# A graph-attention kernel: dense edge weights as relu(A·B − 1) in PSUM by ScalarE, the units' one-hots by VectorE in one pass

## The reference

```python
hs, hd = h[src], h[dst]
e = jnp.concatenate([hs, hd], axis=1)
a1 = jnp.exp(jax.nn.relu(e @ W_att_1 + b_att_1))          # a2, a3 likewise
att1 = jax.ops.segment_sum(a1, dst, num_segments=N)
avg_a = (a1 / att1[dst] + a2 / att2[dst] + a3 / att3[dst]) / 3.0
m = avg_a * relu(relu(relu(hs @ W_msg_1 + b_msg_1) @ W_msg_2 + b_msg_2) @ W_msg_3 + b_msg_3)
h_neigh = jax.ops.segment_sum(m, dst, num_segments=N) / jnp.maximum(deg, 1.0)
out = relu(jnp.concatenate([h, h_neigh], axis=1) @ W_c1 + b_c1) @ W_c2 + b_c2
x = _layernorm(x + out)
```

## Time and profile before

| | us |
|---|---|
| median of 3 runs (784.7 to 786.55) | 785.11 |
| the profiled execution, its own time | 788.37 |
| its span (first to last instruction) | 784.4 |
| PE busy | 635.0 (81%) |
| DVE busy | 562.6 (72%) |
| ACT busy | 460.2 (59%) |
| POOL busy | 573.6 (73%) |
| mean granted TensorE clock | 0.858 |

### The profile page before, as it was taken

How to read it: one execution, slowest core, us unless ns; L and a number is a source line. 1 busy time by engine, 2 the same in 40 slices (tenths; PEclk the granted TensorE clock), 3 DMA queues, 4 the chain that set the end, 5 groups by cost and what they waited for, 6 DMA issues and landing times.

```text
span 784.4 us, 17056 instructions
## 1 busy us (share of the span) xinstructions
PE 635.0 (81%) x5157; PEld 519.2 (66%) x5157; DVE 562.6 (72%) x1855; ACT 460.2 (59%) x1109; POOL 573.6 (73%) x604
## 2 busy tenths in 40 slices
PE   9951889988878777999998788797778877878775
PEld 5741657764655456899988677685667766767664
DVE  4884587588888787788886666665567777677566
ACT  6566687578655455667765555553365556566533
POOL 7777777777777677777777777777777777777760
PEclk9985596599778776899999989988798988899698
DMA  7974263334862233333433333324344444444321
GB/s 228 252 195 105 66 101 84 71 85 78 69 83 75 54 96 80 83 87 87 88 83 80 78 74 83 73 64 133 66 107 104 104 111 128 104 117 104 89 59 35
DMA packets 83313, 75.69 MB, mean 96 GB/s; under 512 B 35064, under 2 KB 66720, under 8 KB 83216
## 3 DMA queue, kind: packets, MB, share of 16 engines
q0 software_dynamic: 19008, 39.82, 25.8%
q1 hardware_dynamic: 63920, 34.59, 16.3%
q10 hardware_dynamic: 288, 0.13, 0.1%
HBM read 64.94 MB, written 9.52 MB: 95 GB/s over the span
## 4 chain that ended last, share of the span: by engine, by line
PE 33%; POOL 30%; issue 13%; DVE 11%; ACT 6%; DMA 5%; DVEq 1%; SPq 0%; POOLq 0%; ACTq 0%
POOL work L1247 30%; PE bank L1434 8%; PE bank L1473 7%; PE bank L1457 4%; PE bank L1440 2%; DVE counts L1730 2%; ACT fin L1578 2%; DVE acc L1907 2%; PE bank L592 2%; PE bank L613 2%; PE bank L1391 1%; DVE fin L1717 1%; PE bank L601 1%; DMA message_table<-work 1%; PE bank L1419 1%
## 5 line engine op out<-in xcount | busy, mean ns | idle before, releaser
L1247 POOL DMA_INDIRECT work<-message_table,src_t x554 | 531.6, 960 | 174.2 <-issue 164.9
L1434 PE MATMUL bank<-work 128*128 128x144 f32 (+8 forms) x1188 | 188.5, 314 | 37.9 <-DVE acc L1907 37.8
L1434 PEld LDWEIGHTS bank<-work 128*128 128x128 f32 x1188 | 174.3, 223 | 50.8 <-issue 43.8
L1604 ACT COPY work<-bank 128x192 f32<-128x192 f32 (+7 forms) x126 | 37.4, 297 | 177.4 <-DVE work L1859 176.0
L1473 PE MATMUL bank<-shared,fin 128*128 128x129 f32 (+1 forms) x882 | 115.1, 286 | 0.0
L1907 DVE TENSOR_TENSOR acc<-acc,bank 128x192 f32 (+8 forms) x297 | 89.1, 300 | 27.4 <-issue 3.6
L1473 PEld LDWEIGHTS bank<-shared,fin 128*128 128x128 f32 (+1 forms) x882 | 106.1, 197 | 2.5 <-issue 0.6
L1890 DVE TENSOR_TENSOR work<-bank,work 128x576 f32<-128x576 f32 (+7 forms) x126 | 86.2, 684 | 13.1
L1765 DVE SCALAR_TENSOR_TENSOR fin<-logits_or_x,per_node,counts 128x384 f32<-128x384 f32 (+1 forms) x147 | 85.8, 611 | 1.9 <-PE bank L1473 1.9
L904 PE MATMUL bank<-rest_w,acc 128*128 128x128 f32 x294 | 52.3, 344 | 40.5 <-DVE fin L995 31.0
L904 PEld LDWEIGHTS bank<-rest_w,acc 128*128 128x128 f32 x294 | 46.5, 246 | 43.0 <-DVE fin L995 32.3
(11 more groups left out here) (162 smaller groups left out, 840.4 us busy)
## 6 DMA issues: line engine op xcount, KB each, us to landing
work<-message_table,src_t POOLq DMA_INDIRECT x554
side<-near_nodes SPq DMA_DIRECT2D x102, 48.0 KB
side<-logit_parts SPq DMA_DIRECT2D x297, 0.8 KB
message_table<-work SPq DMA_DIRECT2D x12, 262.0 KB, 4.7
work<-message_table SPq DMA_DIRECT2D x48, 65.5 KB
work<-in_x_t SPq DMA_DIRECT2D x12, 256.0 KB, 4.9
fin<-in_x SPq DMA_DIRECT2D x11, 256.0 KB, 3.0
logits_or_x<-in_x_t SPq DMA_DIRECT2D x11, 256.0 KB, 3.7
```

The lines of the kernel that those rows point to most:

```text
L1247: pool.indirect_dma_start(out=rows_of(n)[:, t, :], out_offset=None, in_=table[:, :], in_offset=bass.IndirectOffsetOnAxis(ap=src_t[:, h, g: ...
L1434: pe.matmul(sums[:, at:at + HEADS * w], rows_here[:, t, 0:P], wt_of(i)[:, t, :], start=h == 0, stop=h == TILES - 1)
```

## The change

What a hot edge's weight is made of is split another way. ACT computes relu(A·B − 1) for one block and head, 128 x 384 values, into a PSUM bank (`hot_excess`, bank 4, one place only); DVE reads that bank, adds `ok_col` and multiplies by the counts. Since relu(A·B − 1) + 1 = max(A·B, 1), the rows need no scaling: PE takes them as they were loaded, `scale_rows` is gone, and so is the reciprocal. SP's `load_block` now waits for PE's matmuls four blocks back (`s_hm`). All one-hots of the first pass are made by DVE (`by_dve` is true for every unit), also those of units 26 to 125.

```diff
-        inverse = per_node_flat[:, 0:n_blocks * HEADS].rearrange("p (b k) -> p b k", k=HEADS)
...
-        shared = sb("shared", [P, TWO * HEADS * (P + 1)])
-        hot_scaled = shared[:, :].rearrange("p (j k f) -> p j k f", j=TWO, k=HEADS)
+        SHARED = 5 * P
+        shared = sb("shared", [P, SHARED])
...
+                dve.memset(less_one[:, :], -1.0)
+                dve.memset(shared[:, COLS:SHARED], 0.0)
...
             def by_dve(i):
 
-                return first and i < HOT_AT
+                return first
...
                     def load_block(b):
                         if b >= BLOCKS:
-                            sp.wait_ge(s_hr, HEADS * (b - BLOCKS + 1))
+                            sp.wait_ge(s_hm, b - BLOCKS + 1)
...
-                        pe.wait_ge(s_hr, HEADS * (b + 1))
+                        rows_here = hot_block[0:m, b % BLOCKS, 0:1 + P]
+                        pe.wait_ge(s_hb[b % BLOCKS], 16 * (b // BLOCKS + 1))
                         for k in range(HEADS):
                             pe.wait_ge(s_hw, HEADS * b + k + 1)
                             for h in range(HOT):
                                 last = pe.matmul(bank[SIDE_BANKS[h]][:, k * (P + 1):(k + 1) * (P + 1)],
                                                  hot_wt[0:m, b % THREE, k, h * P:(h + 1) * P],
-                                                 hot_scaled[0:m, b % TWO, k, :],
-                                                 start=False, stop=b == n_blocks - 1 and k == HEADS - 1)
+                                                 rows_here, start=False, stop=b == n_blocks - 1 and k == HEADS - 1)
...
-                    def scale_rows(b):
...
-                        for k in range(HEADS):
-                            act.activation(hot_scaled[0:m, b % TWO, k, :], hot_block[0:m, b % BLOCKS, 0:1 + P], ACT.Copy,
-                                           scale=powers[0:m, b, k:k + 1]).then_inc(s_hr, 1)
+                    def hot_excess(b, k):
+
+                        m, n = block_nodes(b), HEADS * b + k
+                        if n == 0:
+                            act.wait_ge(s_hl, 16 * (HEADS * HOT + 1))
+                            act.wait_ge(s_cadd, n_hot)
+                            act.wait_ge(s_ok, OK_STEPS)
+                        else:
+                            act.wait_ge(s_hw, n)
+                        act.activation(bank[EXP_BANK][0:m, 0:hot_nodes], hot_b[0:m, k, :], ACT.Relu, bias=less_one[0:m, 0:1],
+                                       scale=powers[0:m, b, k:k + 1]).then_inc(s_hr, 1)
...
                     for i in range(n_steps):
+                        if first and 0 <= i - HOT_AT - 1 < n_blocks:
+                            hot_excess(i - HOT_AT - 1, 1)
                         if i + 1 < n_units:
                             mask_copy(i + 1)
                             exps(i + 1)
...
                         if first and 0 <= i - HOT_AT - 1 < n_blocks:
-                            scale_rows(i - HOT_AT - 1)
+                            hot_excess(i - HOT_AT - 1, 2)
+                        if first and 0 <= i - HOT_AT < n_blocks:
+                            hot_excess(i - HOT_AT, 0)
...
                     def hot_weights(b, k):
                         m = block_nodes(b)
-                        if b == 0 and k == 0:
-                            dve.wait_ge(s_hl, 16 * (HEADS * HOT + 1))
-                            dve.wait_ge(s_cadd, n_hot)
-                            dve.wait_ge(s_ok, OK_STEPS)
+                        dve.wait_ge(s_hr, HEADS * b + k + 1)
                         if b >= THREE:
                             dve.wait_ge(s_hm, b - THREE + 1)
-                        dve.scalar_tensor_tensor(hot_wt[0:m, b % THREE, k, :], hot_b[0:m, k, :], inverse[0:m, b, k:k + 1],
-                                                 counts[0:m, b, :], ALU.max, ALU.mult).then_inc(s_hw, 1)
+                        dve.scalar_tensor_tensor(hot_wt[0:m, b % THREE, k, :], bank[EXP_BANK][0:m, 0:hot_nodes], ok_col[0:m, 0:1],
+                                                 counts[0:m, b, :], ALU.add, ALU.mult).then_inc(s_hw, 1)
...
-                        known(dve.reciprocal(inverse, powers[:, :, 0:HEADS]))
```

15 lines of the change are left out of this document (5 added, 10 removed).

## The result

The changed kernel takes **806.7 us** (median of 6 runs, 802.0 to 810.2), the kernel before, timed beside it, 783.7 (6 runs, 781.3 to 786.6): a ratio of 1.029, 95% interval 1.0249 to 1.0332. It is slower, by 23 us. Its profiled execution is the shortest of its six (802.0, span 798.2), that of before was longer than all six of its timed ones (788.4, span 784.4), so the two traces differ by 13.8 us only.

The account below looks back on a forecast made before the run. POOL's gathers were taken to bound the kernel, with DVE's longer dense step becoming slower than them. Unit 76 35.4 us later, less 12 worked off, plus 0.2 in the tail, on 785.1 gave 808.7 us; range 786 to 823.

Parts of the forecast that it names:

- D and the step: Dense stage: D, ACT's instruction for one excess, 0.65 us; DVE's step 3.18 + 3 D, 5.13 us at width 32.
- rival 1: Dense stage: mean DVE step under 4.70 to 4.90 us, gathers stay the bound, 779.7 us, faster; chance 0.11.
- The dense stage: Units 31 to 76 (within steps 27 to 75): 233.6 us against 199.2, DVE slower than the gathers' 4.99 a unit.
- The start: Before unit 31: slower steps +1.3 us, reciprocal saves 1.1, three early one-hots cost 0.8; unit 76 35.4 us later.
- The one-hots after that: Final stage: one DVE one-hot a step, 0.27 us each over 47 steps, 12.7 us, hidden by no wait.
- What is worked off: Final stage: DVE's vanished waits for gathers, less one-hots, give back 0 to 21.3 us; 12 taken, PE being next.
- The sign of being wrong that the prediction gave itself: Final stage: forecast wrong if DVE's waits for gathers vanish without PE getting busier.
- The sum: Whole kernel: 35.4 − 12 = +23.4 us, plus 0.2 for the last one-hot in the tail; 808.7 us.
- rival 2: Dense stage: mean step 4.95 us, +24 at unit 76, 20 of it worked off, 789 us; chance 0.14.
- Rival 3: Final stage: nothing worked off, PE and DVE hold each other up; 820.5 us, up to 825 with one-hots; chance 0.20.
- Rival 4: Gathers stay the bound and 100 one-hots on DVE slow them by 0.09 us each, +9, 794 us; chance 0.03.
- The second rule that the prediction took from there: Gathers beside DVE: a `tensor_scalar` in a two-port mode contends with GpSimd reading SBUF, so one-hots would disturb gathers.

Follow-up runs that it names:

- e1: Changed kernel with the one-hots of units 26 and later made by ACT again instead of DVE; 800.6 us, ratio 1.022 to the kernel before.
- e3: Changed kernel with head 1's excess placed behind the unit's mask copy and exp in ACT's list; 786.0 us, ratio 1.004 to the kernel before.
- e7: Changed kernel with ACT computing only 128 of the excess's 384 columns; 780.5 us, ratio 0.994 to the kernel before.
- e4: Changed kernel with the excess put in two SBUF places in turn instead of one in PSUM; 794.8 us, ratio 1.014 to the kernel before.
- e8: Kernel before with the one-hots from unit 78 on made by DVE, those of units 26 to 77 by ACT; 784.3 us, ratio 1.001.
- e6: Kernel before with one extra DVE copy of 192 columns out of PSUM, read by nobody, in each dense step; 792.0 us, ratio 1.009.
- e5: Changed kernel with head 1's excess behind copy and exp, and late one-hots on ACT in two split passes; 779.8 us, ratio 0.996 to the kernel before.
- e2: Kernel before with all one-hots made by DVE and nothing else changed; 792.8 us, ratio 1.015.

## Why the prediction was right, and where it was not

808.7 was forecast, 806.7 measured, by the mechanism that was named: the single place makes DVE's step longer than four gathers. How near the number came is luck in part, as the sum shows. Point by point:

- **D and the step: right.** D was 0.65 and is 0.675, DVE's instruction 0.61 and is 0.614, the step 5.13 and is 5.12; widths 36, 40, 44 gave 5.19, 5.25, 5.32 (5.18, 5.23, 5.28). The one-hot is hidden in the wait for head 2 (e1), the order of ACT's list accounts for 0.38 (e3, 0.36 expected), and the sum 3.18 + 3 D holds for another D (e7, 4.49 against 4.56). D was put at 0.65 between rows; the 0.46 of rival 1 is an estimate for a source in PSUM, where here the result goes there, and a result in PSUM came 0.03 us sooner than one in SBUF (675 and 702 ns, e4).
- **The dense stage: 233.6 said, 238.4 measured.** What the sum left out: every eighth step L1908 waits half a microsecond more, for nothing that the profile shows, and a few other steps lose 0.1 to 0.4 us. The eighth step is where the code loads the starts of the next 16 windows (`REGS`) into registers; that this is the wait I only infer. The step that I took as the sample had none of it. One such step of the changed kernel:

```profile
389.51 0.74 DVE L1908 TENSOR_TENSOR acc<-acc,bank 128x144 f32 x2 [0.64 <-issue]
```

- **The start: wrong, by the profile it was read from.** Unit 31 was to come 1.0 us later and came 5.9 earlier. The profiled execution of before was late there: its granted PE clock from 50 to 150 us was 0.67, in the changed kernel 0.73, in e8, which does the same work up to there, 0.74. Before, e8 and the changed kernel:

```profile
50.00:150.00 100.00, 67.83 (x494) 51.47 (x495) 66.04 (x251) 72.30 (x162) 76.13 (x79) 0.67 0.44 93
```

```profile
50.00:150.00 100.00, 65.63 (x538) 49.46 (x537) 69.17 (x259) 74.72 (x167) 75.91 (x80) 0.74 0.47 97
```

```profile
50.00:150.00 100.00, 66.69 (x539) 50.42 (x538) 70.23 (x264) 75.16 (x168) 76.15 (x79) 0.73 0.46 97
```

  e8, whose time is that of before, has unit 31 at 313.84 and unit 76 at 516.19. Against it the changed kernel is 3.3 and 39.3 us later, where 1.0 and 35.4 were said. But the start scatters: unit 31 comes at 323.0, 312.5 and 313.8 in the three traces with the same work up to there (before, e6, e8), and at 317.1 and 319.2 in the two of the changed kernel. So whether 3.3 is more than 1.0 can't be told.
- **The one-hots after that: mis-sized.** 12.7 us were put down as work. DVE's busy time differs by 15.5, and taken away they give 6.6 in the stage (e1); the rest is covered by the waits shown at e1.
- **What is worked off: the step that failed.** I took 12 of 21.3 us, since PE was busy 5.17 of 5.30 us in the window of the earlier trace rows with the 2.40 us of wait of the earlier trace rows behind it. It gave 21.3 (23.2 against e8), all that DVE had: in e8, with the same one-hots on DVE, L1865 waits 20.9 us for gathers in this stage, and in the changed kernel not at all. PE was hardly in the way: DVE waits for it 1.1 + 1.1 us in the whole stage, where e8 has 5.2 for L1859. That about half of the waited time stands in windows where PE is full was read off a single window. A full window shows that PE is busy, not that its work has to be done then; the matmuls of the stage took 171.4 us here instead of 184.2, at a granted clock of 0.93 instead of 0.87, so that PE was busy 80% of the stage where it had been 78%. The sign of being wrong that the prediction gave itself, that the waits vanish without PE getting busier, is as good as met in this step.
- **The sum.** The number is right by errors that cancel. Against e8's trace (span 780.3, its time equal to its median) the changed kernel's is 17.9 us longer: 39.3 at unit 76 (35.4 said), 23.2 worked off (12 said), 1.8 more in the tail (0.2 said). To this come the 4.7 us by which its median lies above the profiled execution, which no step of mine had, and which is not explained: 22.6 in all, against 23.6 said and 23.0 measured.
- **Rival 1, "the chain is short enough": the deciding point was right.** A mean step (units 31 to 76) of 4.70 to 4.90 us was to decide; the changed kernel has 238.4/45 = 5.30. e7, which leaves out part of the work, has 211.3/45 = 4.70 and is faster, at 780.5 (779.7 was said); e3 has 222.5/45 = 4.94, the 4.95 of rival 2, and is 0.4% slower (786.0, where rival 2 said 789); e5, with the same 4.94, is faster; its final stage has no late one-hots on DVE, which gave 6 us in e1. The gain of unheld gathers, 4.4 + 1.0 us, agrees with e5: its last gather ends 5.7 us before that of e8.
- **Rival 3 and the range.** Nothing worked off was refuted by the 21.3 us. Its upper price and the range don't quite follow from the sums: the one-hots in full on top of 820.5 are 833, not 825; 786 is 808.7 with its terms at their low ends (785.7), not the 789 of rival 2, and 823 is below the high ends (827.7).
- **Rival 4: given 0.03, with the right price and the wrong place.** 9 us for one-hots on DVE is what e2 measured (9.4). The one-hots do hold gathers, but by 1.0 us in all in the changed kernel, and the 9 us of e2 come from the weight instructions, once the step is longer. I had dismissed it by the 948 ns of a stretch in which no weight instruction runs: a mean of 73 gathers hides a few held ones (in the trace of before 4 gathers end by an L1817, 0.3 us together), and it couldn't show what a longer step does beside L1765. Nor did I see in the earlier trace rows that 3.78 us is three gathers and a bit (3 x 1.25 = 3.75).

On the port: the traces show a gather held by L1765, L1772 and by L1004 (128x512, both inputs in SBUF, 4 of 4 in the changed kernel). The Trainium skill (SBUF — State Buffer, Who interferes with whom) says that an instruction with two SBUF inputs contends with GpSimd's reads, and infers that descriptor generation, which writes, isn't stalled by it. None held under L1767, with one input in SBUF, agrees. The 50 held gathers of e2 agree with the first half if what is held is the gather's reading of its row numbers (`src_t`, in SBUF), and speak against the inference if it is the descriptors; no run separates the two. The second rule that the prediction took from there, that `tensor_scalar` in a two-port mode contends too, is borne out by the 13 gathers held by one-hots.

## What to carry to other kernels

A single buffer between two engines makes their instructions add up (here 3.18 + 3 D): count the handovers per step and compare the sum with the pace that bounds the kernel, before asking which engine is busier. Here the order of one list decided (20 us for one moved call), and work placed in a wait that exists anyway is free, while the same work elsewhere is paid.

An engine far from its limit can still slow the bound one if it holds something that the other needs at a fixed point. Compare their periods: here a DVE step a little longer than three gathers, with an instruction in it that holds a gather, locked the gathers to it, and 0.17 to 0.26 us more in the step raised the mean gather from 973 to between 1018 and 1040 ns.

Before reading a start time off one profile, look at the granted clock of that stretch, or have a second execution of the same work to set beside it.

## What the runs showed of the hardware

- A gather issued by POOL is held by a DVE weight instruction with both tensors in SBUF that runs from the gather's start to beyond 0.12 us, and ends 0.82 us behind that instruction's end: 1.24 us in the row of e4, where a free one takes 0.944 (four exceptions in the kernel before and e6). With one input in PSUM it isn't: of 144 that met L1767 in the changed kernel and e1, none.
- The one-hot (`tensor_scalar`, bf16, SBUF to SBUF) holds gathers by the same rule: 13 in the changed kernel, the longest 1.07 us, 1.0 us in all.
- ACT's relu with scale and bias over 384 columns takes 675 ns into PSUM and 702 into SBUF (e4), over 128 columns 461 (e7): 0.84 ns a column, against 0.83 in the earlier trace rows.
- The one-hot on DVE, 48x512, takes 352 to 379 ns in the mean of a kernel, and took 0.52 us once (e3, at 355.22), which is not explained.
- DVE's weight instruction costs the same with its input in PSUM (614 ns) as in SBUF (611); what the place changes is whether gathers are held.
